# Sorting tokens by expert through DRAM in a four-stage transformer kernel

## The chip, the cores and the metric

The kernel runs on 1 core of one Trainium2 chip. The metric is the device time of one execution in microseconds (us), the median of several runs. The core has five engines with a queue of their own each: TensorE (PE in the rows; PEld is its weight load), VectorE (DVE), ScalarE (ACT), GpSimd (POOL) and SyncE (SP), which here only issues DMAs. A queue is worked off in order; engines wait for each other by semaphores.

## The reference

Input `x` is 64 sequences of 64 tokens of 128 numbers in float32, 4096 tokens in all, with a context of the same shape. Four residual sublayers follow each other, the last with the experts:

```python
x = x + tanh(g_xattn[0]) * L0_xattn(layernorm(x), ctx, ctx)        # 16 heads of 8, squared scores
x = x + tanh(g_ffn[0])   * L0_ffn(layernorm(x))                    # FP4-rounded gate/up/down, width 352
x = x + tanh(g_xattn[1]) * L1_xattn(layernorm(x), ctx, ctx, mask)  # one head, softmax
x = x + tanh(g_ffn[1])   * L1_ffn(layernorm(x))

def L1_ffn(src):
    x = ln(src + attention(src), ln1_g, ln1_b)       # 16 heads of 8, softmax
    gates = softmax(x @ gW + gb)                     # 8 experts
    w = the two largest gates of each token, 0 for the other six
    h = relu(einsum('nd,edf->enf', x, W1) + b1)      # 8 experts, 128 -> 256
    y = einsum('enf,efd->end', h, W2) + b2           # 256 -> 128
    return ln(x + einsum('ne,end->nd', w, y), ln2_g, ln2_b)
```

So only two of eight experts count for a token; which two depends on the data.

## The kernel before

**Groups and stages.** The 4096 tokens are worked in 8 groups of 512 (`N`), each four tiles (`T`) of 128 tokens. A group passes through stages whose names begin with a letter for their part: `a_` the first cross-attention, `f_` the FP4 feed-forward, `c_` the second cross-attention, `s_` the self-attention, the gate and the ranking, `e_` the experts and the output. Each engine has a function for each stage that it has a part in. The work of several groups is interleaved: a table `ORDER` at the end of the file lists, for each of the five queues, every stage with its group, as `e_hid.3:5` (piece 3 of group 5). This order is written out; nothing is decided at run time. Entries `w.N:0` of TensorE's list are fillers: N transposes of the identity into bank H, for no result (315 to 379 of them in the two kernels).

**Banks.** PSUM is cut into A2, A1 (parts a and f), B2, B1 (parts c and s), H and Y (the experts). `claim`, `filled` and `freed` turn a stage's place in TensorE's list into the semaphore value that a writer or a reader of its bank waits for.

**The norms.** Each of six norms per group takes four `bn_stats` on VectorE (`moments`), eleven small instructions on GpSimd (`factors`, one of them a power), and four activations on ScalarE (`normal`).

**The experts (dense).** `s_gate` computes gate logits, `s_rank` the softmax and for each token the rank of each expert, and `wgt`, the gate where the rank is 0 or 1 and 0 elsewhere. `s_gt` turns `wgt` for the product with the biases. Then each group goes through all 8 experts: `e_hid` k (16 of them) multiplies a half of an expert's first matrix, resident in `w1_s`, with all 512 tokens into H, and ScalarE takes it out with bias and relu into `hid`; `e_out` e makes 8 matmuls of 128 x 128 into Y, and VectorE adds them into `acc`, scaled by the token's weight for this expert:

```python
mm(H[:], w1_s[:, e, P * c:P * c + P], xmT[:, g % 2])                         # e_hid, 512 columns
mm(Y[:, P*t:P*t+P], hid[:, e % 2, c, P*t:P*t+P], w2_s[:, e, c, :], c == 0, c == FCH - 1)   # e_out
ve.scalar_tensor_tensor(out=acc[..t..], in0=Y[..t..], scalar=wgt[.., t, e:e+1], in1=acc[..t..], mult, add)
```

After the last expert follow the sixth norm (`e_n6`), a product on GpSimd (`e_z`), the sum with the residual (`e_fin`) and the store (`e_o`). A float32 matmul is two instructions in the profile, a transpose one. All matmuls go through one helper (L957), all plain ScalarE copies and activations through another (L468); so rows are told apart by their tiles. `pool` in the rows is the buffer that holds `hid` and `acc`.

Of the kernel before, what the change touches and what calls it, by code (L numbers as in the profile page):

```python
# [23 lines left out]
def flamingo_gated_stack(nc, x, ctx_in, mask, g_xattn, g_ffn,  # L24
# [6 lines left out]
    T = 4  # L31
# [15 lines left out]

    def tiles(ap):
        return ap.rearrange("b s d -> (b s) d").rearrange("(t p) d -> p t d", p=P)

    x_v, c_v, m_v, o_v = tiles(x), tiles(ctx_in), tiles(mask), tiles(out)

    ctx = ExitStack()
    with ctx:
# [15 lines left out]
        w1_s = sb("w1_s", [E, FCH * P])  # L70
# [37 lines left out]
        xax = sb("xax", [XB]); xsc = sb("xsc", [XB]); xrc = sb("xrc", [XB]); xqm = sb("xqm", [N])  # L108
# [3 lines left out]
        hqm = sb("hqm", [WID])  # L112
        th = sb("th", [2, I]); hh = sb("hh", [T, I])
        hqT = sb("hqT", [3, N])
# [5 lines left out]
        xs = sb("xs", [2, T, P])  # L120
        stats3 = sb("stats3", [T, 6]); hs3 = sb("hs3", [3, T]); rstd3 = sb("rstd3", [2, T])
        xn3 = sb("xn3", [T, P]); xT3 = sb("xT3", [N])
        q1T = sb("q1T", [N]); k1T = sb("k1T", [N]); v1s = sb("v1s", [T, P])
        keep = sb("keep", [T, S]); fill = sb("fill", [T, S])
# [6 lines left out]
        xT4 = sb("xT4", [N])  # L131
# [11 lines left out]
        xm = sb("xm", [T, P]); xmT = sb("xmT", [2, N]); wgt = sb("wgt", [2, T, E]); wT = sb("wT", [P])  # L143
        xb = sb("xb", [T, P])
        pool = sb("pool", [2 * FCH * N + 2 * N])
        hid = pool[:, 0:2 * FCH * N].rearrange("p (a c n) -> p a c n", a=2, c=FCH)
        acc = pool[:, 2 * FCH * N:2 * FCH * N + 2 * N].rearrange("p (a t d) -> p a t d", a=2, t=T)
# [34 lines left out]
        set1 = dict(A2=B2, A1=B1, qk=xmT[:].rearrange("p a (t d) -> p a t d", t=T), A0=P4, kT0=qT4, hT0=hT4,  # L182
# [7 lines left out]
        def bank_of(stage, g):  # L190
            b = BANK[stage]
            return {"A2": "B2", "A1": "B1"}[b] if stage[0] == "a" and g in OTHER else b

# [9 lines left out]
        setup = signal("setup"); p_b2 = signal("p_b2"); vset = signal("vset"); tanh = signal("tanh"); v_wq = signal("v_wq")  # L203
        x_wq = signal("x_wq"); x_qx = signal("x_qx"); x_qh = signal("x_qh")
        LOADS_W, LOADS_B, LOADS_O, LOADS_G, LOADS_F, LOADS_1, LOADS_E = 3, 3, 2, 2, 7, 18, 9
# [19 lines left out]
        v_out = signal("v_out")  # L225

# [14 lines left out]
        for stage, k, g in order("TensorE"):  # L241
            if stage in BANK and (stage, k) not in JOINED:
                bank_ = bank_of(stage, g)
# [4 lines left out]
        def claim(pe, stage, g, k=0):  # L248

            after(pe, free[bank_of(stage, g)], FREED[stage, k, g] - READERS.get(stage, 1))  # L250

        def filled(engine, stage, g, k=0):

            if g >= 0:
                engine.wait_ge(full[bank_of(stage, g)], FILLED[stage, k, g])

        def freed(engine, stage, g, k=0):

            if g >= 0:
                engine.wait_ge(free[bank_of(stage, g)], FREED[stage, k, g])  # L260
# [1240 lines left out]
```

## Time and profile before

| | |
|---|---|
| median of 3 runs | 723.52 us (722.88 to 726.53) |
| span of the profiled execution | 724.5 us (the page gives no other time for it) |
| TensorE busy | 673.4 us, 93% |
| VectorE busy | 516.0 us, 71% |
| ScalarE busy | 408.5 us, 56% |
| GpSimd busy | 265.6 us, 37% |
| DMA | 12.72 MB, mean 18 GB/s |

Busy times of different engines overlap. A row of the groups of instructions has: line, engine, operation, tile written <- tiles read, shape, count, then the busy time of the group and the mean duration of one, then the idle time of the engine ahead of it with what ended it. For TensorE the mean is longer than the step from one instruction to the next, since they are pipelined; the chain of waits shows the steps.

### The profile page before, as it was taken

Reading aid. Unit: us, or ns where it says so; the run is one execution under the profiler, and the core shown is the slowest. Engines: PE = TensorE matmul, PEld = TensorE weight load, DVE = VectorE, ACT = ScalarE, POOL = GpSimd, SP = SyncE. Lnnn points to the kernel's source line nnn. Section 1 sums busy time; section 2 is a strip of 40 time slices with the busy share of each in tenths; the row PEclk is TensorE's granted clock in tenths of the full one; section 3 lists DMA queues with packets and bytes.
Section 4 is the critical chain, followed back from the end, with each engine's and each line's share of the span. In section 5 each row is a group of like instructions: output and inputs, shape, how many; then the busy total and the mean of one; then the engine's idle time right before and its main releaser. Section 6 shows DMA issues by size and latency. Waiting matters only on the chain.

```text
span 724.5 us, 19854 instructions
## 1 busy us (share of the span) xinstructions
PE 673.4 (93%) x8416; PEld 496.8 (69%) x8416; DVE 516.0 (71%) x1085; ACT 408.5 (56%) x680; POOL 265.6 (37%) x624
## 2 busy tenths in 40 slices
PE   6898889998999999999999999999999999998983
PEld 6777676676677776777777777677676667566552
DVE  0928745997968787988897868878889765674432
ACT  2353665456755675758666765475747474644331
POOL 6023531085226335452455334352524125113202
PEclk8989999999999999999999999999999999999997
DMA  5510000100000010000000000000000000000000
GB/s 152 155 53 2 2 2 2 30 3 23 24 3 1 2 44 24 3 2 1 24 2 15 3 2 25 1 2 2 10 17 1 2 10 8 1 16 1 1 15 15
DMA packets 24023, 12.72 MB, mean 18 GB/s; under 512 B 6432, under 2 KB 23424, under 8 KB 23936
## 3 DMA queue, kind: packets, MB, share of 16 engines
q1 hardware_dynamic: 21888, 10.52, 5.3%
q8 instruction: 67, 1.10, 0.6%
q10 hardware_dynamic: 2048, 0.94, 0.5%
q14 instruction: 20, 0.16, 0.1%
HBM read 9.36 MB, written 2.10 MB: 16 GB/s over the span
## 4 chain that ended last, share of the span: by engine, by line
PE 78%; DVE 9%; ACT 6%; POOL 3%; issue 2%; DMA 1%; ACTq 1%; POOLq 0%; SPq 0%; DVEq 0%
PE B L957 18%; PE A L957 17%; PE Y L957 17%; PE H L957 15%; PE B L1214 4%; PE A L961 2%; PE B L961 2%; ACT pool L468 1%; ACT A L468 1%; PE A L1110 1%; POOL hs L366 1%; ACT xn L473 1%; DVE stats L680 1%; DVE hax L660 1%; DMA y<-in_L_xattn_Wq_w_dram 1%
## 5 line engine op out<-in xcount | busy, mean ns | idle before, releaser
L957 PE MATMUL H<-xmT,w_s 128*128 128x512 f32 x256 | 135.4, 611 | 6.4 <-ACT pool L468 6.4
L957 PEld LDWEIGHTS Y<-w_s,pool 128*128 128x128 f32 x1024 | 121.4, 192 | 20.2 <-issue 15.8
L468 ACT ACTIVATE pool<-H,b_s 128x512 f32<-128x512 f32 x128 | 87.7, 685 | 82.8 <-PE H L957 82.1
L957 PE MATMUL Y<-w_s,pool 128*128 128x128 f32 x1024 | 126.6, 277 | 2.5 <-ACT pool L468 1.6
L934 DVE SCALAR_TENSOR_TENSOR pool<-Y,wgt,pool 128x128 f32<-128x128 f32 x256 | 71.8, 343 | 46.8 <-PE Y L957 46.6
L356 POOL TENSOR_TENSOR hs<-stats 128x4 f32<-128x4 f32 x48 | 13.3, 278 | 237.1 <-DVE stats L680 236.9
L957 PEld LDWEIGHTS H<-xmT,w_s 128*128 128x128 f32 x256 | 40.0, 190 | 26.3 <-ACT pool L468 15.3
L875 DVE TENSOR_REDUCE mx<-B 128x16 f32<-128x1024 f32 x32 | 39.0, 1220 | 24.9 <-PE B L957 24.8
L966 PE MATMUL H<-ident 128*128 128x128 f32 x379 | 51.1, 286 | 1.7 <-POOL ident L341 1.7
L957 PE MATMUL B<-hT,qT 32*64 32x256 f32 (+1 forms) x640 | 47.6, 374 | 4.3 <-ACT P L468 1.0
L366 POOL TENSOR_TENSOR hs<-hs,mhalf 128x4 f32<-128x4 f32 x48 | 49.8, 1037 | 3.8
L966 PEld LDWEIGHTS H<-ident 128*128 128x128 f32 x379 | 45.4, 148 | 4.7 <-issue 2.6
L957 PE MATMUL A<-wguT,xTq 128*128 128x352 f32 x128 | 45.7, 481 | 2.0 <-DVE hh L783 1.8
L468 ACT ACTIVATE PT<-B 128x1024 f32<-128x1024 f32 x32 | 32.7, 1021 | 21.9 <-PE B L1214 21.8
L405 POOL TENSOR_TENSOR hh<-hh,hsc 128x1408 f32<-128x1408 f32 x6 | 15.5, 2589 | 77.1 <-DVE hh L673 77.1
L957 PE MATMUL A<-hT,kT 32*64 32x128 f32 x896 | 38.6, 283 | 4.5 <-ACT A L468 2.2
L468 ACT ACTIVATE P<-P 128x1024 f32<-128x1024 f32 x32 | 33.6, 1052 | 14.9 <-DVE P L877 14.9
L468 ACT ACTIVATE A<-A 128x1024 f32<-128x1024 f32 x28 | 28.6, 1021 | 20.9 <-PE A L957 20.9
L877 DVE TENSOR_TENSOR P<-B,mx 128x1024 f32<-128x1024 f32 x32 | 39.2, 1225 | 1.1
L957 PEld LDWEIGHTS A<-hT,kT 32*64 32x64 f32 x896 | 25.2, 132 | 19.4 <-PE A L957 6.8
L957 PEld LDWEIGHTS B<-hT,qT 32*64 32x64 f32 x640 | 17.2, 130 | 26.9 <-PE B L957 10.5
L882 DVE RECIPROCAL rc<-B 128x256 f32<-128x256 f32 x16 | 28.1, 1755 | 9.2 <-PE B L957 9.1
(232 smaller groups left out, 1371.0 us busy)
## 6 DMA issues: line engine op xcount, KB each, us to landing
xin<-in_x_dram SPq DMA_DIRECT2D x8, 256.0 KB, 3.6
out_dram<-xb SPq DMA_DIRECT2D x8, 256.0 KB, 2.3
cin<-in_ctx_dram SPq DMA_DIRECT2D x7, 256.0 KB, 3.0
w_s<-in_L_ffn_W_dram SPq DMA_DIRECT2D x1, 1024.0 KB
min_<-in_mask_BxSxS_ik_dram SPq DMA_DIRECT2D x8, 128.0 KB, 2.4
cin<-in_ctx_dram ACTq DMA_DIRECT2D x1, 256.0 KB, 4.3
hh<-in_L_ffn_w_down_dram ACTq DMA_DIRECT2D x1, 176.0 KB, 5.5
hh<-in_L_ffn_w_gate_dram ACTq DMA_DIRECT2D x2, 64.0 KB, 5.4
```

Source lines behind the costliest of these rows:

```text
L356: pl.tensor_tensor(w[:, 0], st[:, :, 1], st[:, :, 4], ALU.subtract)
L366: pl.tensor_tensor(w[:, 0], w[:, 0], mhalf[:], ALU.pow).then_inc(p_n[k], 1)
L405: pl.tensor_tensor(h, h, rep(hsc[:, 0:QB], 2, BLK), ALU.mult).then_inc(p_qh, 1)
L468: return act.activation(dst, source, f, **kw)
L875: ve.tensor_reduce(mx4[:, t % 2], by_s, AX.X, ALU.max).then_inc(v_mx, 1)
L877: ve.tensor_tensor(P4[:, t % 2].rearrange("p (h s) -> p h s", s=S), by_s, rep(mx4[:, t % 2], 2, S), ALU.subtract).then_inc(free["B2"], 1)
L882: ve.reciprocal(rc4[:], B1[:, N // 2:N]).then_inc(v_rc, 1)
L934: last = ve.scalar_tensor_tensor(out=acc[:, g % 2, t, :], in0=Y[:, P * t:P * t + P], scalar=wgt[:, g % 2, t, e:e + 1], in1=acc[:, g % 2, t ...
L957: return pe.matmul(o, l, r, start=start, stop=stop)
L961: last = pe.transpose(dst[:, P * t:P * t + P], source[:, t, :], ident[:])
L966: pe.transpose(H[:, 0:P], ident[:], ident[:])
L1214: last = pe.transpose(B2[:, P * pr:P * pr + P], P4[:, t % 2, a:a + P], ident[:])
```

## The change

The experts are computed only for the tokens that chose them. A group of 512 tokens makes 1024 token-expert pairs. They are sorted by expert into slots in DRAM, each expert's share beginning at a new tile of 128 slots; at most 15 tiles are needed, and always 15 are worked (`TILES`). `PARTS` says which groups are sorted together; here every group is by itself. Step by step:

- `i_cnt` (TensorE) counts, with products of 0/1 matrices, how many earlier tokens chose each expert; `s_rank` writes the 0/1 choices for it, and the two weights per token (`wk`).
- `i_pos` (VectorE, 17 small instructions) turns the counts into slot numbers `pos` and into the expert that owns each tile, `own`, and gathers its bias `b1t`.
- `i_sc` (GpSimd) writes each token's row of `xm` to its two slots: 8 indirect DMAs of 128 rows per group. `i_x` (SyncE) loads the sorted rows back, four tiles (a quad) at a time.
- `i_w` (SyncE) reads a tile's expert from `own` into a register and loads this expert's first matrix (128 KB) into one of 8 buffers (`w1t`); the resident `w1_s` is gone. The second matrices stay resident and are addressed by a register.
- `m_x` transposes a quad (TensorE, ScalarE), `m_h` makes the hidden layer, `m_y` the output; ScalarE copies it to SBUF and SyncE stores it to DRAM slots.
- `e_g` (GpSimd) gathers each token's two results: 8 indirect DMAs per group. `e_cmb` (VectorE) adds them, weighted, in place in `xm` (four buffers, `KEEP`). In the last group `m_` stages use two more banks in turn.
- To make room, several buffers are shared or single now: `xs`, `xT3` with `xT4`, `hqm` with `hqT`, `fill` with the mask, `xmT` with `xT0`. The residual of the output (`xs` plus a bias) goes out to DRAM (`r_st`) and comes back for `e_fin` (`r_ld`). Many stages get waits for the last reader of the buffer that they overwrite.
- The queues' orders are written anew. SyncE's list grows from 34 to 233 entries, GpSimd's from 104 to 165; TensorE's fillers go from 379 to 315.

The core of the diff:

```diff
+    TILES = [(2 * n * P + E * (P - 1)) // P for n in TG]
+    QUADS = [(n + 3) // 4 for n in TILES]
+    slots_x = [nc.dram_tensor("slots_x%d" % c, [TLM * P, D], F32) for c in range(2)]
+    slots_y = [nc.dram_tensor("slots_y%d" % c, [TILES[c] * P, D], F32) for c in range(CHUNKS)]
...
-        w1_s = sb("w1_s", [E, FCH * P])
+        w1t = sb("w1t", [NW, FCH * P])
...
+                def r_st(g, k):
+                    sp.wait_ge(p_xb, g + 1)
+                    sp.dma_start(r_v[:, g * T:g * T + T, :], xs[:]).then_inc(s_res, 16)
...
+                def i_w(c, j):
...
+                    e = sp.value_load(own[0:1, c % 2, j:j + 1], min_val=0, max_val=E - 1)
+                    sp.dma_start(w1t[:, n % NW, :], w1[bass.ds(e, 1)].rearrange("e d f -> d (e f)")).then_inc(ld_wt[n % NW], 16)
...
+                def i_x(c, q):
...
+                    sp.wait_ge(ld_sc[c], 32 * TG[c])
...
+                    sp.dma_start(xg[:, n % 2, 0:nt, :], slots_x[c % 2][4 * q * P:(4 * q + nt) * P, :].rearrange("(t p) d -> p t d", p=P))\
+                        .then_inc(ld_xg[n % 2], 16)
...
+                def m_y(c, q):
...
+                    sp.dma_start(slots_y[c][4 * q * P:(4 * q + nt) * P, :].rearrange("(t p) d -> p t d", p=P), yq[:, n % 2, 0:nt, :])\
+                        .then_inc(s_yq[n % 2], 16)
...
+                def i_sc(c, t):
...
+                    for k in range(2):
+                        pl.indirect_dma_start(out=slots_x[c % 2][:, :], out_offset=bass.IndirectOffsetOnAxis(ap=pos[:, c % 2, k, t:t + 1], axis=0),
+                                              in_=xm[:, g % KEEP, t % T, :], in_offset=None).then_inc(ld_sc[c], 16)
...
+                def e_g(g, t):
...
+                    for k in range(2):
+                        pl.indirect_dma_start(out=yg[:, k, t, :], out_offset=None, in_=slots_y[c][:, :],
+                                              in_offset=bass.IndirectOffsetOnAxis(ap=pos[:, c % 2, k, at_:at_ + 1], axis=0)).then_inc(ld_yg, 16)
...
-                def e_hid(g, k):
-                    e, c = divmod(k, FCH)
-                    filled(act, "e_hid", g, k)
-                    copy(hid[:, e % 2, c, :], H[:], ACT.Relu, bias=b1_s[:, e, c:c + 1]).then_inc(free["H"], 1)
+                def m_h(c, p):
...
+                    for j in range(2 * p, min(2 * p + 2, TILES[c])):
+                        for h in range(FCH):
+                            at_ = 2 * P * (j % 2) + P * h
+                            last = copy(hid[:, n % 2, j % 4, h, :], m_bank("m_h", c, p)[:, at_:at_ + P], ACT.Relu,
+                                        bias=b1t[:, c % 2, h, j:j + 1])
...
-                def e_out(g, e):
-                    filled(ve, "e_out", g, e)
+                def e_cmb(g, k):
...
+                    ve.wait_ge(ld_yg, 16 * 2 * T * (g + 1))
+                    for h in range(2):
+                        after(ve, v_cmb, 2 * g + h)
+                        for t in range(T):
+                            last = ve.scalar_tensor_tensor(out=xm[:, g % KEEP, t, :], in0=yg[:, h, t, :],
+                                                           scalar=wk[:, c % 2, h, first + t:first + t + 1],
+                                                           in1=xm[:, g % KEEP, t, :], op0=ALU.mult, op1=ALU.add)
...
+                def m_x(c, q):
+                    n = FIRST_Q[c] + q
+                    if q == 0:
+                        pe.wait_ge(v_i, INDEXED * c + INDEXED)
+                    for j in range(min(4, TILES[c] - 4 * q)):
+                        at_ = 4 * q + j
+                        owners[n % 2, j] = pe.value_load(own[0:1, c % 2, at_:at_ + 1], min_val=0, max_val=E - 1)
+                    pe.wait_ge(ld_xg[n % 2], 16 * (n // 2) + 16)
+                    claim(pe, "m_x", c, q)
...
+                            last = mm(m_bank("m_h", c, p)[:, at_:at_ + P], w1t[:, i % NW, P * h:P * h + P],
+                                      xgT[:, n % 2, P * (j % 4):P * (j % 4) + P])
...
+                            last = mm(m_bank("m_y", c, q)[:, P * j:P * j + P], hid[:, n % 2, j, h, :], w2_s[:, bass.ds(owners[n % 2, j], 1), h, :],
+                                      h == 0, h == FCH - 1)
...
+PARTS = ((0,), (1,), (2,), (3,), (4,), (5,), (6,), (7,))
```

The new TensorE queue ends, from the last attention output (`s_o4:7`) on: `m_x:6 e_bias:6 m_h:6 s_n5t:7 m_x.1:6 s_gate:7 m_h.1:6 m_y:6 m_x.2:6 i_cnt:7`, the rest of group 6's tiles with `s_gt:7` among them, then all tiles of group 7 and `e_bias:7`.

## Rows read from the trace of the kernel before

**Rows 1.** The page: span, busy time by engine.
```profile
span 724.5 us, 19854 instructions
...
PE 673.4 (93%) x8416; PEld 496.8 (69%) x8416; DVE 516.0 (71%) x1085; ACT 408.5 (56%) x680; POOL 265.6 (37%) x624
```

**Rows 2.** The page: chain that ended last, by engine and by line.
```profile
PE 78%; DVE 9%; ACT 6%; POOL 3%; issue 2%; DMA 1%; ACTq 1%; POOLq 0%; SPq 0%; DVEq 0%
PE B L957 18%; PE A L957 17%; PE Y L957 17%; PE H L957 15%; PE B L1214 4%; PE A L961 2%; PE B L961 2%; ACT pool L468 1%; ACT A L468 1%; PE A L1110 1%; POOL hs L366 1%; ACT xn L473 1%; DVE stats L680 1%; DVE hax L660 1%; DMA y<-in_L_xattn_Wq_w_dram 1%
```

**Rows 3.** Busy time by stretch: engines, granted TensorE clock, DMA share, GB/s.
```profile
0.00:20.00 20.00, 14.41 (x103) 13.07 (x104) 3.62 (x11) 4.16 (x9) 10.96 (x25) 0.83 0.57 147
...
60.00:100.00 40.00, 34.25 (x435) 27.21 (x434) 28.33 (x49) 23.62 (x41) 15.23 (x41) 0.96 0.01 1
...
300.00:400.00 100.00, 99.75 (x1281) 73.27 (x1281) 83.15 (x178) 66.85 (x119) 44.42 (x105) 1.00 0.03 8
...
680.00:724.00 44.00, 27.57 (x155) 18.60 (x154) 11.85 (x39) 12.00 (x21) 8.85 (x21) 0.92 0.04 12
```

**Rows 4.** Chain of waits in order of time: start, us, what; 640 to 725 us.
```profile
705.34 0.70 ACT pool L468
706.04 0.04 issue
...
707.21 1.78 PE Y L957 x16
708.99 0.88 PE H L957 x2
```

**Rows 5.** Groups of instructions on TensorE: hidden, output, fillers.
```profile
L957 PE MATMUL H<-xmT,w_s 128*128 128x512 f32 x256 | 135.4, 611 | 6.4 <-ACT pool L468 6.4
L957 PE MATMUL Y<-w_s,pool 128*128 128x128 f32 x1024 | 126.6, 277 | 2.5 <-ACT pool L468 1.6 <-DVE pool L934 0.9
L966 PE MATMUL H<-ident 128*128 128x128 f32 x379 | 51.1, 286 | 1.7 <-POOL ident L341 1.7
```

**Rows 6.** Groups on ScalarE and VectorE, shapes apart.
```profile
L468 ACT ACTIVATE pool<-H,b_s 128x512 f32<-128x512 f32 x128 | 87.7, 685 | 82.8 <-PE H L957 82.1
L473 ACT ACTIVATE xn<-xr,rstd 128x128 f32<-128x128 f32 x32 | 13.2, 484 | 12.1 <-POOL rstd L370 12.1
L468 ACT ACTIVATE xmT<-B 128x512 f32<-128x512 f32 x8 | 4.7, 593 | 4.1 <-PE B L961 4.1
L468 ACT ACTIVATE woT<-A 128x128 f32<-128x128 f32 x1 | 0.3, 259 | 0.0
L923 DVE SCALAR_TENSOR_TENSOR wgt<-rank,pe_ 128x32 f32<-128x32 f32 x8 | 1.5, 192 | 0.3
```

**Rows 7.** Group on VectorE: accumulation of an expert's output.
```profile
L934 DVE SCALAR_TENSOR_TENSOR pool<-Y,wgt,pool 128x128 f32<-128x128 f32 x256 | 71.8, 343 | 46.8 <-PE Y L957 46.6
```

**Rows 8.** Groups on GpSimd: the power in the norms, the longest instruction.
```profile
L366 POOL TENSOR_TENSOR hs<-hs,mhalf 128x4 f32<-128x4 f32 x48 | 49.8, 1037 | 3.8
L405 POOL TENSOR_TENSOR hh<-hh,hsc 128x1408 f32<-128x1408 f32 x6 | 15.5, 2589 | 77.1 <-DVE hh L673 77.1
```

**Rows 9.** DMA issues with landing; an issue's own time; a table load.
```profile
xin<-in_x_dram SPq DMA_DIRECT2D x8, 256.0 KB, 3.6
out_dram<-xb SPq DMA_DIRECT2D x8, 256.0 KB, 2.3
...
2.29 0.43 SPq L300 DMA_DIRECT2D y<-in_L_xattn_Wq_w_dram  x1
...
10.84 1.28 ACT L465 ACT_TABLE_LOAD   x1 [10.84 <-issue]
```

**Rows 10.** Timeline: last attention output, end of the ranking, last statistics.
```profile
660.40 1.06 PE L957 MATMUL B<-wdir,oT 128*128 128x128 f32 x8
...
677.33 0.19 DVE L923 SCALAR_TENSOR_TENSOR wgt<-rank,pe_ 128x32 f32<-128x32 f32 x1
...
713.88 0.87 DVE L680 BATCH_NORM_STATS2 stats<-pool 128x6 f32<-128x128 f32 x4
```

More of the change, by code:

```diff
@@ L46, in flamingo_gated_stack @@
     MAGIC = 1.5 * 2.0 ** 22
+    CHUNKS = len(PARTS)
+    PART = {g: c for c, part in enumerate(PARTS) for g in part}
+    TG = [T * len(part) for part in PARTS]
+    TILES = [(2 * n * P + E * (P - 1)) // P for n in TG]
+    QUADS = [(n + 3) // 4 for n in TILES]
+    FIRST = [sum(TILES[:c]) for c in range(CHUNKS)]
+    FIRST_Q = [sum(QUADS[:c]) for c in range(CHUNKS)]
+    TGM, TLM = max(TG), max(TILES)
+    LOADS_Z = 2 * ((TLM + 15) // 16)
+    KEEP = 4
+    NW = 8
     def tiles(ap):
@@ L510, in a_qt @@
                 def a_qt(g, k):
+                    if g == 0:
+                        act.wait_ge(vset, 3)
+                    filled(act, "a_s0", before(g), T - 1)
                     filled(act, "a_qt", g)
@@ L518, in a_av @@
                 def a_av(g, k):
+                    filled(act, "a_o0", before(g))
                     filled(act, "a_av", g)
@@ L582, in c_pt @@
                 def c_pt(g, k):
+                    filled(act, "c_av", g - 1)
+                    if g == 0:
+                        act.wait_ge(v_l2, norms(OTHER[0] + 1))
                     filled(act, "c_pt", g)
@@ L695, in a_k @@
                 def a_k(g, k):
+                    filled(ve, "a_kt", before(g))
+                    filled(ve, "a_qt", before(g))
                     filled(ve, "a_kv", g)
@@ L717, in a_q @@
                 def a_q(g, k):
+                    filled(ve, "a_kt", before(g))
+                    filled(ve, "a_qt", before(g))
                     filled(ve, "a_q", g)
@@ L824, in c_p @@
                 def c_p(g, k):
+                    filled(ve, "c_pt", g - 1)
                     ve.wait_ge(x_c, g + 1)
@@ L872, in s_s @@
                 def s_s(g, t):
+                    filled(ve, "s_t", *((g, t - 2) if t > 1 else (g - 1, t + 2)))
+                    if g == 0 and t == 0:
+                        filled(ve, "a_av", OTHER[0])
                     by_s = B2[:].rearrange("p (h s) -> p h s", s=S)
@@ L880, in s_o @@
                 def s_o(g, p):
+                    filled(ve, "s_o4", g - 1)
+                    if g == 0 and p == 0:
+                        filled(ve, "a_o0", OTHER[0])
                     filled(ve, "s_av", g, 2 * p)
@@ new lines, in i_cnt @@
+                def i_cnt(c, k):
+                    n = TG[c]
+                    skip = TGM - n
+                    pe.wait_ge(v_g, 16 * PARTS[c][-1] + 13)
+                    if c == 0:
+                        pe.wait_ge(p_ix, 7)
+                    claim(pe, "i_cnt", c)
+                    mm(Y[:, 0:n * E + E], before_m[:], flat(picked[:, skip:TGM + 1, :]), True, False)
+                    for t in range(n):
+                        last = mm(Y[:, (t + 1) * E:(n + 1) * E].rearrange("p (t e) -> p t e", e=E), ones_m[:],
+                                  rep(picked[:, skip + t, :], 1, n - t), False, t == n - 1)
+                    last.then_inc(full["Y"], 1)
@@ new lines, in m_y @@
+                def m_y(c, q):
+                    n = FIRST_Q[c] + q
+                    nt = min(4, TILES[c] - 4 * q)
+                    freed(pe, "m_h", c, (4 * q + nt - 1) // 2)
+                    claim(pe, "m_y", c, q)
+                    for j in range(nt):
+                        for h in range(FCH):
+                            last = mm(m_bank("m_y", c, q)[:, P * j:P * j + P], hid[:, n % 2, j, h, :], w2_s[:, bass.ds(owners[n % 2, j], 1), h, :],
+                                      h == 0, h == FCH - 1)
+                    last.then_inc(full[bank_of("m_y", c, q)], 1)
```

651 lines of the change are left out of this document (417 added, 234 removed).

## The prediction

> **What bounds the kernel now.** I read the page first. The span is 724.5 us, and the engines' busy times are 673.4 (TensorE), 516.0 (VectorE), 408.5 (ScalarE) and 265.6 (GpSimd) [rows 1]. The chain that ended last is 78% TensorE, and two banks of one helper line, Y and H, hold 17% and 15% of it [rows 2]: these are the expert matmuls. The stretches say when that holds. Between 300 and 400 us TensorE is busy 99.75 of 100 us and VectorE 83; from 60 to 100 us TensorE has only 34.25 of 40, and in the last 44 us 27.57 [rows 3]. So in the body what counts is TensorE work, and at the end a chain through all engines counts. The profile gives the span alone as its execution's time; the sum below is made against 724.5, which is 1.0 above the median of the runs (723.52).
>
> **What the experts cost.** For each group, every token goes through all 8 experts: 16 hidden matmuls of 512 columns and 64 output matmuls of 128 columns, each float32 matmul being two instructions. In the chain a hidden one (x2) takes 0.88 us and one expert's output (x16) 1.78 us, so one instruction of 128x128 by 128 columns takes 0.111 us at full clock [rows 4]. The chain's shares for Y and H on the helper line, 17.3% and 15.4%, are 237 us; less the bias products, 8 of the hidden shape at 0.87 = 7, the experts are 230 us. (The groups' own busy times, 126.6 and 135.4, include ends that lie under the next instruction [rows 5].)
>
> **After the change, per group.** 512 tokens x 2 choices in tiles that belong to one expert need at most 15 tiles, where the dense form has 32 tile-expert pairs. 15 tiles x (2 hidden + 2 output) x 2 instructions = 120, of the shape of the output matmuls: 13.3 us. 15 transposes at 0.13 (51.1 / 379 [rows 5]): 2.0. The count of positions, five small products, ten instructions at 0.1: 1.0. Together 16.3, for 8 groups 130. The queue has 315 fillers where there were 379, 64 x 0.135 = 8.6 less. Net TensorE: -230 + 130 - 8.6 = **-108.6 us**.
>
> **The other engines.** ScalarE loses 87.7 and gains, per group, 30 small activations at some 0.33 (between 0.259 and 0.484 [rows 6]), 4 copies in at 0.59 and 4 out at 0.59: 14.6 x 8 = 117, so 438 in all. VectorE loses 71.8 (256 accumulations at 0.28) and gains per group 8 accumulations at 0.28, five more small steps in the ranking and 17 in the placing at 0.19 [rows 6, 7], 6.4 in all: 516 - 72 + 51 = 495. Neither passes TensorE's 565, but in the 561 us up to the last attention output (below) VectorE now has about 480 to do, so an order of the queues that leaves gaps costs more than now. GpSimd gets 128 indirect DMAs (8 out, 8 back per group). The trace has none. Below stands a DMA issue on a hardware queue, 0.43 us [rows 9]; above, GpSimd's longest instruction, 2.59 [rows 8]. I take 1.04, the row of its slow small operation, since an indirect DMA is also work per partition in software: 128 x 1.04 = 133, GpSimd 399 in all, not the bound. But 8 of them in a row hold back what is queued behind them, above all the norms' factors, for which ScalarE and then TensorE wait; 8.3 us of such a hold costs nothing while another group's work lies in the queues, and that cover is thin at both ends.
>
> SyncE gets 120 expert loads of 128 KB, 32 tile loads, 32 tile stores, 16 transfers of the residual and 2 of zeros, about 202 issues x 0.43 = 87 us, and its queue waits in order. The bytes are 15.7 (weights) + 2 x 7.9 (tiles) + 8.4 (rows by index) + 4.2 (residual) + 2 (zeros) = 46 MB, 69 GB/s over 667 us; the first 20 us carry 147 GB/s [rows 3], so bandwidth is hidden. Single buffers in place of double ones (xs, xT3 with xT4, hqm with hqT, the mask with its fill) and the added waits for a reader cost nothing as long as the body is paced by TensorE; the residual must be stored before the next one is written, 1.3 + 2.3 us, under the fourth stage's attention.
>
> **Register loads.** Both TensorE and SyncE now read the tile's expert number into a register, 120 times each, and TensorE's queue waits behind each. The trace has no such load. Below stands the chain's gap of 0.04 us; above, the table load of ScalarE, 1.28, the only instruction here that fetches state; next below it a DMA issue at 0.43 [rows 4, 9]. I take 0.2, nearer to the issue, since four stand in a row and earlier matmuls still run: 24 us (bounds 5 and 154).
>
> The Trainium skill (DMA: Bandwidth & Descriptors, Latency and other measured facts) gives a load into registers a floor of about 600 ns, which unrolling by four amortizes. With 0.6 for each of 120 the estimate by that page is 72 us in place of 24, and the total 715; no row here shows it.
>
> **The end, step by step.** The last group's attention output leaves TensorE at 661.5 us, and 191 of the 230 us of expert work lie ahead of it (21 hidden and 11 output pieces, 39 us, behind). After: 661.5 - 191 + 6 groups x 16.3 + 1 - 8.6 = 561. From there to the end of the ranking the trace shows 661.5 to 677.5, 16.0 us [rows 10]. Then the count 1.1, nine placing steps 2.5, eight scatters 8.3, landing 2.3, the load of the tiles 3.6 [rows 9]: 34 us, of which TensorE fills only the 15.3 of group 6 and about 2 more. Then the experts of group 7, alone: TensorE 15.3, ScalarE 14.6, partly in turns, as the chain shows them now (0.70 of ScalarE between TensorE's pieces [rows 4]): 22. Then copy 0.6, store 2.3, eight gathers 8.3, landing 2.3, accumulations 2.2, and what follows now from the statistics at 713.9 to the end, 10.6 [rows 10]: 26.3. Sum: 561 + 34 + 22 + 26.3 = 643.3; with the register loads 667.3, against the runs' median **about 667**. So 57 us are gained, not 109: 27 are eaten by the way through DRAM at the end, 24 by the register loads.
>
> On landing, the Trainium skill (same page, Anatomy of one DMA) gives about 2.0 us plus the bytes at 436 GB/s, 2.2 for 64 KB as an estimate; the stores' 2.3 for 256 KB is near it, the loads' 3.6 above. That would leave the sum within 1 us.
>
> **The rivals.** (a) *The forecast*, 667, with its own range 635 to 700: chance 0.45. (b) *The register loads stall TensorE* at the price of the table load: 643 + 154 = 797. It decides from (723.5 - 643.3) / 120 = 0.67 us each; above that the kernel is slower. For it: a queue that waits for a fetch does nothing else. Against it: TensorE's own queue runs ahead by some instructions and the loads come before a wait anyway. Chance 0.13. (c) *GpSimd paces the body*: at 2.59 us per indirect DMA it has 265.6 + 332 = 597 us of work and the two ends grow by 16 x 1.55 = 25, so 692 at least; each group's six chains of factors (now 1.04 + eight small steps) queue behind 20 us blocks, and 8 x 4 us of that exposed gives 725. For it: GpSimd's waits are long today only because it is early. Chance 0.15. (d) *TensorE's work goes but the span doesn't follow*: VectorE at 495 us, more small dependent steps, a SyncE queue in order, single buffers. If the body packs like 60 to 100 us (0.86) and not like 300 to 400 (1.00), the 561 us become about 610, total 716; half of that, 690. Chance 0.17. (e) *Better than the sum*: loads at 0.04 and the early third, now 0.86 to 0.96 full, filled by the new order: 620 to 640. Chance 0.10. The granted clock is a part of all: it was 0.83 and 0.92 at the two ends, where TensorE was less busy [rows 3]; if the last 22 us of experts ran at 1.2 GHz, 15 us more.
>
> **Numbers.** Likeliest 667. Below 620 and above 728 I leave 0.04 and 0.15, so the range is 620 to 728. A change under 0.5% (3.6 us) can't be told from none here. Faster: all of (a) and (e), most of (d), half of (c), a little of (b): 0.77; same 0.04; slower 0.19.
>
> **What would show it.** TensorE busy near 565 us with 960 expert instructions at some 0.111 each; gaps of TensorE before the tile transposes in fours (register loads), 0.8 us if I am right, over 2.7 if (b); GpSimd's indirect DMAs at about 1 us each (over 2 if c), total near 400; a gap of TensorE of some 15 us ahead of the last group's experts and 26 us behind them; VectorE near 495. The prediction is wrong if TensorE's share of the chain falls under 60% in the body.

## The result and the profile after

The changed kernel takes **816.5 us** (median of four runs, 814.6 to 826.0); the kernel before, on the same chip, 725.0. The ratio is 1.128, 95% interval 1.122 to 1.135. The prediction was 667, range 620 to 728: the change makes the kernel 13% slower, not 8% faster, and the time lies outside the range.

The page of the changed kernel, to be read against [rows 1] and [rows 2]. In the slices, each digit is the busy share of 20.4 us in tenths, and for PEclk the granted clock:

```profile
span 816.4 us, 21791 instructions
...
PE 641.0 (79%) x8232; PEld 507.4 (62%) x8232; DVE 506.9 (62%) x1069; ACT 424.5 (52%) x856; POOL 413.1 (51%) x759
...
PE   3787988998988899989999889687876777666720
...
PEclk9979999999999999999679999979779899568775
...
PE 47%; DVE 18%; issue 11%; ACT 9%; POOL 8%; DMA 3%; SPq 1%; POOLq 0%; DVEq 0%; ACTq 0%
```

Three engines' busy times stand there nearly as priced: VectorE 507 (495), ScalarE 425 (438), GpSimd 413 (399). TensorE was to be busy near 565 us and is busy 641, 32 us less than before, at a mean granted clock of 0.891 instead of 0.983. The two products, 673.4 x 0.983 = 662 and 641.0 x 0.891 = 571, are a rough estimate of the work at full clock: some 91 us of it went (predicted 108.6). But TensorE's share of the chain fell from 78 to 47%, and "issue", time in which an engine waits for nothing that is shown, rose from 2 to 11%. The work went, and the span grew.

Where it grew is told by one marker, VectorE's reading of the last group's attention output. It came at 661.56 before. Here the marker stands at

```profile
709.38 0.69 DVE L1100 TENSOR_TENSOR y<-B,src 128x512 f32<-128x512 f32 x1 [2.26 <-PE B L1229]
```

**So the body, all that lies ahead of this marker, was to be 76 us shorter and is 48 us longer; the end, all behind it, grew from 63 to 107 us.** The stretches of the changed kernel (columns as in [rows 3]) show a TensorE that is never full and a clock that falls:

```profile
300.00:400.00 100.00, 89.38 (x1173) 70.79 (x1171) 75.64 (x152) 62.97 (x130) 49.59 (x77) 0.96 0.30 86
...
500.00:600.00 100.00, 80.53 (x820) 62.53 (x818) 59.18 (x126) 51.44 (x112) 54.67 (x78) 0.88 0.29 84
600.00:709.00 109.00, 78.50 (x1016) 64.72 (x1008) 53.56 (x135) 48.28 (x111) 50.09 (x86) 0.83 0.34 97
709.00:816.00 107.00, 51.01 (x299) 44.17 (x297) 25.73 (x81) 34.48 (x99) 43.97 (x72) 0.69 0.37 106
```

The costliest groups of the change (busy, mean ns of one, idle before and its releaser); the expert groups answer to [rows 5, 6], L1233 are the transposes of the tiles, L554 and L566 scatter and gather:

```profile
L566 POOL DMA_INDIRECT yg<-slots_y,pos x64 | 62.5, 977 | 42.9 <-issue 39.3
L1229 PE MATMUL H<-xgT,w1t 128*128 128x128 f32 x452 | 71.2, 305 | 14.6 <-ACT pool L597 9.0
L597 ACT ACTIVATE pool<-H,b1t 128x128 f32<-128x128 f32 x226 | 64.8, 370 | 33.8 <-PE H L1229 33.1
L554 POOL DMA_INDIRECT slots_x<-xm,pos x64 | 63.6, 994 | 35.4 <-issue 18.6
...
L1229 PE MATMUL Y<-w_s,pool 128*128 x452 | 66.6, 309 | 2.7 <-ACT pool L597 2.6
...
L1233 PE MATMUL H<-ident,xg 128*128 128x128 f32 x113 | 21.5, 318 | 48.1 <-issue 39.2
```

Ahead of these 113 transposes (the other seven of the 120 write bank A) TensorE is idle for 48.1 us in all, 39.2 of it "issue". That is where the four register loads of a quad stand. One such gap of 2.27 us in the timeline of TensorE:

```profile
449.07 0.63 PE L1229 MATMUL B<-PT,ones 128*32 128x64 f32 x32
451.97 0.30 PE L1233 MATMUL H<-ident,xg 128*128 128x128 f32 x1 [2.27 <-issue]
```

Four causes stood open. L: the register loads stall TensorE. C: the clock falls where TensorE waits, and that costs the time. H: a chain of waits that leads each group through all engines holds the body, whatever TensorE has to do. O: the changed order with its waits is slow in itself. G, a smaller one, is GpSimd's blocks of indirect DMAs.

### The profile page after: what moved, and what is told of

Same layout as the page of the kernel before. It is cut to its first block, busy times and chain, and to the rows that moved or that the text cites. A ratio compares the mean times of both kernels' runs of the same rounds, so it can differ in the third digit from the quotient of the medians.

```text
span 816.4 us, 21791 instructions
## 1 busy us (share of the span) xinstructions
PE 641.0 (79%) x8232; PEld 507.4 (62%) x8232; DVE 506.9 (62%) x1069; ACT 424.5 (52%) x856; POOL 413.1 (51%) x759
## 3 DMA queue, kind: packets, MB, share of 16 engines
q1 hardware_dynamic: 82192, 47.11, 20.4%
## 4 chain that ended last, share of the span: by engine, by line
PE 47%; DVE 18%; issue 11%; ACT 9%; POOL 8%; DMA 3%; SPq 1%; POOLq 0%; DVEq 0%; ACTq 0%
PE B L1229 13%; PE A L1229 12%; PE Y L1229 6%; PE H L1229 5%; ACT pool L597 3%; PE B L1486 3%; PE H L1233 2%; DVE mx L1081 2%; POOL hs L458 2%; DVE stats L870 2%; DVE P L1083 2%; ACT hT L614 1%; PE A L1233 1%; PE B L1233 1%; DVE rc L1091 1%
## 5 line engine op out<-in xcount | busy, mean ns | idle before, releaser
L566 POOL DMA_INDIRECT yg<-slots_y,pos x64 | 62.5, 977 | 42.9 <-issue 39.3
L1229 PE MATMUL H<-xgT,w1t 128*128 128x128 f32 x452 | 71.2, 305 | 14.6 <-ACT pool L597 9.0
L597 ACT ACTIVATE pool<-H,b1t 128x128 f32<-128x128 f32 x226 | 64.8, 370 | 33.8 <-PE H L1229 33.1
L554 POOL DMA_INDIRECT slots_x<-xm,pos x64 | 63.6, 994 | 35.4 <-issue 18.6
L1229 PEld LDWEIGHTS H<-xgT,w1t 128*128 128x128 f32 x452 | 62.7, 213 | 25.0 <-ACT pool L597 11.8
L1229 PE MATMUL Y<-w_s,pool 128*128 x452 | 66.6, 309 | 2.7 <-ACT pool L597 2.6
L1229 PEld LDWEIGHTS Y<-w_s,pool 128*128 128x128 f32 x452 | 63.6, 224 | 5.7 <-issue 5.1
L1233 PE MATMUL H<-ident,xg 128*128 128x128 f32 x113 | 21.5, 318 | 48.1 <-issue 39.2
L597 ACT ACTIVATE PT<-B 128x1024 f32<-128x1024 f32 x32 | 32.8, 1024 | 45.1 <-PE B L1486 44.7
L1229 PE MATMUL B<-hT,qT 32*64 32x256 f32 (+1 forms) x640 | 48.1, 378 | 7.7 <-ACT PT L597 2.8
L1233 PEld LDWEIGHTS H<-ident,xg 128*128 128x128 f32 x113 | 13.8, 159 | 55.6 <-issue 49.0
L1486 PE MATMUL B<-ident,P 128*128 128x128 f32 x256 | 36.9, 291 | 6.3 <-DVE P L1083 5.5
L597 ACT ACTIVATE A<-A 128x1024 f32<-128x1024 f32 x28 | 28.7, 1024 | 23.3 <-PE A L1229 23.1
L1205 DVE SCALAR_TENSOR_TENSOR xm<-yg,wk,xm 128x128 f32<-128x128 f32 x64 | 21.4, 396 | 30.7 <-DMA yg<-slots_y,pos 29.1
```

Source lines behind the costliest of these rows:

```text
L554: pl.indirect_dma_start(out=slots_x[c % 2][:, :], out_offset=bass.IndirectOffsetOnAxis(ap=pos[:, c % 2, k, t:t + 1], axis=0), in_=xm[:, g ...
L566: pl.indirect_dma_start(out=yg[:, k, t, :], out_offset=None, in_=slots_y[c][:, :], in_offset=bass.IndirectOffsetOnAxis(ap=pos[:, c % 2, k, ...
L597: return act.activation(dst, source, f, **kw)
L1205: last = ve.scalar_tensor_tensor(out=xm[:, g % KEEP, t, :], in0=yg[:, h, t, :], scalar=wk[:, c % 2, h, first + t:first + t + 1], in1=xm[:, ...
L1229: return pe.matmul(o, l, r, start=start, stop=stop)
L1233: last = pe.transpose(dst[:, P * t:P * t + P], source[:, t, :], ident[:])
```

## The experiments

All runs in one table. "Last output" is the marker above, in the profiled execution; the time is the median of the runs. So the two need not fit to the microsecond: the profiled execution of the changed kernel took 818.2 us, and e2's 783.7, e5's 682.9, e6's 696.3 and e13's 718.7, up to 5 us more than their medians. A kernel that lacks or changes part of the result is marked with a star, and its section says which part. The edits below are shown shortened.

| kernel | time | last output | from there to the end of the span |
|---|---|---|---|
| before | 725 | 662 | 63 |
| changed | 816.5 | 709 | 107 |
| e1 static experts in the output product * | 782.2 | 676 | 105 |
| e2 one load a quad, no checks | 778.4 | 679 | 103 |
| e11 one load a quad, with checks | 801.8 | 696 | 106 |
| e4 old order, no experts * | 697.0 | 658 | 38 |
| e5 the same, 4 fillers * | 679.5 | 643 | 38 |
| e6 the same, 12 fillers * | 692.5 | 656 | 39 |
| e9 as e5, no maxima * | 656.6 | 615 | 38 |
| e10 before, no maxima | 724.2 | 659 | 63 |
| e3 new order, no experts * | 723.5 | 678 | 46 |
| e13 the same, no placing * | 715.4 | 671 | 46 |
| e16 as e2, no maxima | 770.7 | 665 | 102 |
| e7 as e2, plain DMAs * | 768.1 | 671 | 95 |
| e8 as e2, no loads on SyncE * | 776.1 | 674 | 103 |
| e12 as e2, fillers at the end | 788.7 | 681 | 105 |
| e14, e15 as e2, light experts * | 781.6, 778.9 | 679, 677 | 101, 100 |
| e17 before, with 64 loads | 731.6 | 666 | 63 |
| e18 before, two banks at the end | 720.9 | 661 | 58 |

**e1: no register loads on TensorE.**

```
-  owners[n % 2, j] = pe.value_load(own[0:1, c % 2, at_:at_ + 1], min_val=0, max_val=E - 1)
+  owners[n % 2, j] = at_ % E          # and w2_s[:, owners[n % 2, j], h, :]
```

> Leaves out the 120 register loads on TensorE: the output product takes expert (tile number mod 8) instead of the tile's owner, so the output differs; everything else, the weight loads on SyncE and their register loads too, is as in the changed kernel. Theory L (the register loads stall TensorE, 49 us of waits ahead of the tiles' transposes, and the stalls let its clock fall): the waits ahead of the transposes fall under 15 us and the kernel takes 740 to 775 us. Rival O (the written order and the chain over SyncE, DRAM and GpSimd pace the kernel, TensorE would only wait elsewhere): 800 us or more, the idle time of TensorE stays above 150 us.

782.2 us, ratio to before 1.078 (1.077 to 1.080): 34 us shorter than the changed kernel, nearly all of it ahead of the last output (709 to 676). The tiles' transposes now wait 4.3 us in all, as L said, but the time lies between the two marks, above L's 775 and below O's 800: the loads are a part, not the cause. The products take another expert's second matrix, so the output differs.

**e2 and e11: one load instruction for four owners, without and with the checks of the bounds.** Both give the results of the changed kernel.

```
+  vals = nc.values_load_multi_w_load_instructions(own[0:1, c % 2, 4 * q:4 * q + nt], engines=[mybir.EngineType.PE],
+             min_val=0, max_val=E - 1, skip_runtime_bounds_check_because="...")[1]      (e11: without skip_...)
```

> The same results as the changed kernel: the four owners of a quad are loaded into TensorE's registers by one load instruction (32 loads in place of 120) and without the instructions that check their bounds (two for each owner). Theory L, if the cost sits in the loads and their checks: 49 us of waits fall to about 15 and the time comes to 770 to 790 us. Rival O: within 10 us of the changed kernel.

> The changed kernel with the four owners of a quad loaded by one load instruction (32 in place of 120), but with the two instructions for each owner that check its bounds left in. If the cost sits in the loads, it takes 778 to 785 us, as the run without the checks; if in the checks, 805 us or more.

778.4 and 801.8 us. From 120 loads to 32: 14.7 us, 0.17 for each load that went. Without the 240 checking instructions: another 23.4 us, 0.10 each. The 32 loads that stay in e2 cost nothing that shows: e1, with none, takes 782.2 us, no less than e2. The group of the tiles' transposes, e11 first, then e2:

```profile
L1233 PE MATMUL H<-ident,xg 128*128 128x128 f32 x113 | 21.7, 321 | 32.4 <-issue 24.7 <-DMA xg<-slots_x 4.8 <-ACT pool L597 2.7
```

```profile
L1233 PE MATMUL H<-ident,xg 128*128 128x128 f32 x113 | 19.6, 297 | 8.1 <-ACT pool L597 4.2 <-issue 2.6 <-DMA xg<-slots_x 0.9
```

The "issue" ahead of them goes 39.2, 24.7, 2.6. Loads and checks are 38 of the 91 us (34 by e1); e11 lay between its two marks, so neither loads nor checks alone are "the" cost. The other 53 us remain.

**e4 and e3: the body without experts, in the old and in the new order.** Taken out of the queues, in e4 the hidden and output products and the accumulations, in e3 scatter, gather, weight and tile transfers, the tile stages and the combining. Both lack the experts in their output.

```
- e_hid.*  e_out.*                             (e4, from before)
- m_x m_h m_y i_w i_x i_sc e_g e_cmb           (e3, from the changed kernel)
```

> The kernel before without its dense experts (no hidden products, no output products, no accumulates; the bias product stays), in the order of before. Its output lacks the experts. 665 us of TensorE's work at full clock less 230 is 435; with the idle time of start and end, 500 to 560 us. It is the measure for the body in the changed order: Theory O has it 40 us or more shorter than that one, theory L within 20.

> The changed kernel without its experts: no scatters, no weight loads, no tile transposes, no products, no gathers, no combining; routing, placing, the bias product and everything before them stay, in the changed order. Its output lacks the experts. TensorE's work left is about 450 us at full clock. Theory O (the order and the added waits are themselves slow): at least 40 us longer than the kernel before without its experts. Theory L: within 20 us of it, near 560 us.

697.0 us for e4 and 723.5 for e3, where 500 to 560 and about 560 were expected. e4 decides. **With no expert work at all, the body of before ends at 658 us instead of 662.** 230 us of TensorE's work go and 4 us come back; the whole is 28 us shorter, 25 of it at the end. TensorE is no longer full then, and its mean clock of 0.81 means that it had the lower of its two levels for 0.38 of the stretch (e4: its last output, then 220 to 640):

```profile
657.67 0.69 DVE L890 TENSOR_TENSOR y<-B,src 128x512 f32<-128x512 f32 x1 [2.24 <-PE B L957]
...
220.00:640.00 420.00, 317.01 (x4300) 220.61 (x4300) 284.20 (x516) 208.52 (x350) 166.53 (x392) 0.81 0.03 8
```

And e3's last output, at 678, is that of e2 and e1 (679, 676): leaving the experts out of the changed body gives nothing either. e3 takes 26.5 us more than e4, 20 of them ahead of the last output: between L's mark (within 20) and O's (40 or more). These 20 us don't build up evenly. Up to the output of the group before the last, e3 is 12 us behind e4 (603.6, 592.0); from there to the last output it loses 9 more. e2 against the kernel before shows the same: 7 us behind at that point (609.4, 602.7), 17 at the last output. In e3 too the clock is low, 0.78 from 220 to 640, and no run adds fillers to that body.

**e5 and e6: is it the clock?** Each hidden product of e4's kernel is replaced by 4 or 12 filler transposes.

```
- e_hid.0:0 ...
+ w.4:0 ...          (e6: w.12:0)
```

> The kernel before with each of its 128 hidden products replaced by four filler transposes of TensorE (512 of them, about 57 us at 0.11 us each), its output products and accumulates left out; its output lacks the experts. Without fillers this body took 697 us, its last attention output left at 658 and TensorE had a half clock for 161 us between 220 and 640. Theory C (the half clock makes the body slow where TensorE has too little to do): the clock comes back, the last attention output leaves before 625 and the kernel takes 640 to 670 us. Rival H (the body is held by the chain of products, reductions, exponentials and copies over the engines, whatever TensorE's load or clock): the last attention output stays at 650 to 662.

> As the run with four fillers, but twelve for each hidden product (1,536 fillers, about 170 us of TensorE, most of what the dense experts took): the clock should be full over the whole body. Theory C: TensorE's work is 435 + 170 = 605 us, so the last attention output leaves about 600 to 630 and the whole takes 650 to 680. Rival H: 650 to 662 for the last attention output, 690 to 700 for the whole, although the clock is full.

679.5 (its runs spread from 670 to 683, and the profiled one is the longest) and 692.5 us. With four the clock rises from 0.81 to 0.91 and the last output comes 15 us earlier; with twelve it is nearly full, 0.98, and the output is at 656 again (e5, then e6, the same stretch):

```profile
220.00:640.00 420.00, 342.70 (x4859) 252.35 (x4857) 290.87 (x521) 211.95 (x353) 169.50 (x394) 0.91 0.03 9
```

```profile
220.00:640.00 420.00, 387.68 (x5468) 316.87 (x5467) 287.13 (x523) 210.81 (x352) 167.84 (x395) 0.98 0.03 9
```

So the rise to 0.91 is worth 15 us or somewhat more in that body. e5's last output, 643, lies between the marks of C (before 625) and H (650 to 662); e6 is where H has it. Theory C falls as the main cause. What a full clock without fillers would give isn't shown, since the fillers take time of TensorE's queue themselves; e5's fastest run, 670.2 us at a mean clock of 0.933, suggests some microseconds more.

**e9 and e10: which chain?** The 32 reductions on VectorE that take the row maxima of the second attention are left out; zero is subtracted instead, which leaves the softmax the same up to rounding.

```
- ve.tensor_reduce(mx4[:, t % 2], by_s, AX.X, ALU.max).then_inc(v_mx, 1)
+ (mx4 set to 0 once)
```

> The old body with four fillers in place of each hidden product (680 us, last attention output at 643), without the 32 reductions of VectorE that take each row's maximum before the exponential of the second attention (1.22 us each, 39 us in all; zero is subtracted instead). It lacks the experts, as that run does. If the chain through VectorE sets the pace of the body (rival H), the last attention output leaves 20 to 39 us earlier, at 604 to 623; if something else paces it, under 8 us earlier.

> The kernel before, dense experts and all, without the same 32 maxima (zero is subtracted instead). Its TensorE is busy for 415 of the 420 us between 220 and 640. If TensorE is a second bound at the same place, the time hardly moves: 715 to 726. If TensorE's full row was only filled by what waited anyway, the time falls by 20 us or more, as in the body without experts.

656.6 us: 23 shorter than e5, last output 615 instead of 643. VectorE, busy only 69% of the body of e5 (290.87 of 420 us), stands in the chain that paces it. The same cut in the kernel before gives nothing (724.2, ratio 0.9988, 0.9973 to 1.0003), because there TensorE is full (e10, the same stretch):

```profile
220.00:640.00 420.00, 414.61 (x5191) 301.26 (x5192) 306.58 (x683) 264.94 (x444) 166.46 (x394) 1.00 0.03 9
```

**The body of before has two bounds at nearly the same place:** TensorE's work, and a chain of products, reductions, exponentials and copies that ends at 643 to 658 by itself. Take away either, the other stays. All these runs keep the written order of the attention and feed-forward stages, which was made with the experts in it; whether an order made for the body alone would end earlier wasn't tried.

**e16: the same cut in the sparse kernel** (e2's).

> The kernel of the run with one load a quad (778 us) without the 32 maxima of VectorE before the exponential of the second attention (39 us of VectorE, zero is subtracted instead). In the old body without experts this gave 23 us. If the changed kernel's body is held by the same chain: 15 to 30 us shorter. If it is held by TensorE, the loads or the queues of SyncE and GpSimd: under 8 us.

770.7 us. The last output comes 14 us earlier in the profiled executions (679, 665), but e2's was 5 us above its median; the medians differ by 7.7. That is half of the least that I expected of the chain, and just under the 8 us of its rival. So 39 us less of VectorE give the changed kernel a third of what they give e5's body: this chain is at most one part of what holds it, and the run doesn't say what the rest is.

**e13: the new body without the placing.** It lacks the experts, as e3.

```
- i_cnt (TensorE)   i_pos (VectorE, 17 instructions a group)
```

> The changed kernel's body without experts (723 us, last attention output at 678) also without the placing: the counting products on TensorE and the 16 VectorE instructions a group that turn counts into slots, owners and biases; it lacks the experts as that run does. VectorE is busy 35 us longer there than in the old order's body. If this bookkeeping on the queue of the chain makes the new body 20 us slower: last attention output at 660 to 668, the whole 10 us or more shorter. If the order and the added waits do: within 5 us of 723.

715.4 us, 8 shorter than e3, last output 671 instead of 678: between the two expectations. The runs of both spread (709 to 719, 718 to 726), so the size is rough. The placing, 33 us of VectorE, makes up about 7 of the 20 us; the other 13 are order, shared buffers and waits, which I didn't separate.

**e7 and e8: the queues of GpSimd and SyncE.**

```
- pl.indirect_dma_start(...)                   (e7)
+ pl.dma_start(slots_x[...fixed rows...], xm[:, g % KEEP, t % T, :])
- e = sp.value_load(own[...]); w1[bass.ds(e, 1)]   (e8)
+ w1[j % E]
```

> The kernel of the run with one load a quad (778 us), with each of the 128 indirect DMAs of GpSimd replaced by a plain DMA of the same tile to or from fixed slots, on the same queue; the rows go to other slots than the router says, so the output differs. Rival G (the blocks of eight indirect DMAs, 10 us of GpSimd each, hold the factors of the normalizations and the end): 20 us or more shorter. Theory L and rival O: within 10 us in the body; at the end the scatters and gathers of the last group give back at most 8 us.

> The kernel of the run with one load a quad (778 us), with the weight loads on SyncE issued for expert (tile number mod 8) without a register load: 120 register loads less on SyncE, the 120 weight DMAs stay; the products take another expert's first weights, so the output differs. If SyncE's queue, 1.1 us for each weight load, holds the rows of tokens and the results behind it: 15 us or more shorter, most of it after the last attention output. If not: within 5 us.

768.1 us (10 shorter than e2, half of the least that G asked for) and 776.1 (2 shorter, inside the spread). A plain DMA on GpSimd's queue takes 556 ns of it where the indirect one takes 977 to 994, 56 us less busy in all, and a fifth of that returns. In e7 other rows go through other slots, in e8 the products take another expert's weights.

**e12: the clock at the end.** 390 fillers in TensorE's order from the last cross attention on; results unchanged.

> The kernel of the run with one load a quad (778 us) with 390 filler transposes (43 us of TensorE at full clock) spread over TensorE's order from the last group's cross attention on, three before each attention or routing stage and six before each step of the experts, where TensorE waits and its clock was at half for 81 of the last 142 us. Theory C for the end (half clock doubles the products on the path): 10 to 20 us shorter. If the path is held by copies, transfers and the gathers: within 4 us, or longer by the fillers' own time.

788.7 us: 10 longer. The clock between 640 and 780 rose from 0.72 to 0.90 and the time too. That is the net of two things that this run can't part, what the clock gives back and what the fillers take (estimated at 43 us of TensorE's queue, 390 x 0.11). So C's 10 to 20 us didn't come; that the clock costs nothing at the end isn't shown. e2, then e12:

```profile
640.00:780.00 140.00, 78.57 (x711) 66.16 (x711) 46.74 (x136) 47.19 (x123) 61.51 (x97) 0.72 0.34 98
```

```profile
640.00:780.00 140.00, 95.92 (x1029) 84.43 (x1027) 49.77 (x136) 50.31 (x127) 61.62 (x97) 0.90 0.35 98
```

**e14 and e15: the experts of the last groups made light.** Of group 6, and then of 6 and 7, one hidden product in four, one output product in eight and one copy in four are left; the output of these groups is wrong.

> The kernel of the run with one load a quad (778 us) with the experts of group 6 cut to one product of eight on TensorE and one copy in four on ScalarE, all waits, transposes, loads, scatters and gathers kept; the output of that group is wrong. In its profile group 6's experts lie from 690 to 719 and group 7's transposes start at 719. If they alone hold group 7 back: 15 to 25 us shorter. If group 7's own routing and scatter (placing at 700, scatter 703 to 713, rows loaded about 717) end as late: within 5 us.

> As the run with group 6 cut, with group 7's experts cut in the same way. Group 7's experts took 28 us there (719 to 747), 16 of it products and 17 copies in turn. The cut one should leave about 10 us of transposes, weight and row loads and one copy a step: 15 to 18 us shorter than the run with group 6 alone; if the loads of weights or rows of SyncE set those 28 us, under 6 us shorter.

781.6 and 778.9 us: neither gets clearly shorter than e2's 778.4. Both lie at the mark that has something else hold the end (within 5, under 6). The chain of e15's kernel shows what stands there instead of the products (start, us, what):

```profile
715.14 3.30 DMA slots_y<-pool
718.43 8.40 issue
726.84 1.00 POOL yg L566
...
735.55 0.96 POOL yg L566
736.51 0.30 issue
736.82 2.49 DMA yg<-slots_y,pos
...
745.82 0.17 POOL rstd L462
745.99 0.31 issue
746.30 1.07 POOL yg L566
...
755.18 2.45 DMA yg<-slots_y,pos
```

The last results of group 6 are stored by SyncE only at 722.6, behind weight loads of group 7 and a residual load:

```profile
722.01 0.56 SPq L378 DMA_DIRECT2D xb<-res_d  x1
722.62 0.50 SPq L413 DMA_DIRECT2D slots_y<-pool  x1
```

Then GpSimd gathers group 6 (10 us), waits for the combining and computes group 6's factors, and only then gathers group 7, whose buffer yg is the same. From 726.8 to 757.6 that is 31 us that no faster expert shortens. With full experts, as in e2, the last product's copy ends at 747.5 and group 7's gathers start at 750.4; in e15, without most of the products, they start at 746.3. Two chains end side by side again.

**e17: the price of a load by itself**, in the kernel before, results the same.

```
+ owner = pe.value_load(own_all[0:1, e:e + 1], min_val=0, max_val=E - 1)   # ahead of each output product
- w2_s[:, e, c, :]
+ w2_s[:, bass.ds(owner, 1), c, :]
```

> The kernel before, with the expert of each of its 64 output products taken from a register: one load with two checks and an address of two steps ahead of each, on a TensorE that is busy 99% of the body. Same results. Theory L (a load with its checks is time of TensorE's queue, 0.3 us each by the 38 us of 120): 64 x 0.3 = 19, so 740 to 750 us. Rival: the queue runs ahead of the matmuls in flight and hides them: under 5 us more.

731.6 us, ratio 1.0077 (1.0053 to 1.0102): 5.5 us for 64 loads with their checks, 0.085 each, near the rival's mark and far from L's 19 us. In the waits of TensorE 3.0 us show:

```profile
PE Y L959 <- issue: 3.0, 10, 0.6
```

Singly between long rows of matmuls the same instructions cost a quarter of the 0.32 us that they cost in fours ahead of a transpose. That in the second case the matmuls in flight run out, and in the first not, fits both numbers; no run separates it from other reasons.

**e18: can the end be shortened?** The kernel before with the last group's hidden products in two banks in turn, results the same.

```
+ if stage == "e_hid" and g == GROUPS - 1 and k % 2:
+     return "A1"
```

> The kernel before, with the hidden products of the last group written in turn to two banks of PSUM (H and the one that the attentions no longer use) in place of one. Same results. In the chain of before, seven gaps of 0.78 us after the last attention output wait for the copy that frees the one bank: 7 x 0.78 = 5.5 us shorter, 717 to 721 us. If another chain of the last group (accumulates, norms) takes their place: within 2 us.

720.9 us, ratio 0.993 (0.991 to 0.995): 5.2 shorter, where 5.5 were summed. It beats both kernels.

## Why the prediction was wrong

**The step that failed is the 561:** "661.5 - 191 + 6 groups x 16.3 + 1 - 8.6". It turns TensorE's work into time in the body one for one. [Rows 3] gave the licence, 99.75 busy of 100; but a full row says only that TensorE is a bound, not that nothing else lies just behind. Measured without any expert, the last output comes at 658, four us earlier, where the same sum (661.5 - 191) gives 470. Of the 100 us that the sum took out of the body none came: with the cheap loads of e2 it ends at 679, with the changed kernel's at 709.

The rival for this, (d), "TensorE's work goes but the span doesn't follow", had the right mechanism with a chance of 0.17 and too small a price: I took its packing from another stretch, 0.86, and wrote 610. That doesn't come out of its own numbers: 561 / 0.86 is 652, and 758 in all, which is still 59 us short. Rows of busy time don't give 658 or 678; the chain has to be followed, one group through all engines, or measured without the work.

The terms one by one, against the forecast of 667, 149 us too low:
- **Body, without the loads' cost:** forecast 561, measured 679 (e2, in a profiled execution 5 us above its median): 118 of the 149. That is 17 us above before's own 662; between the two bodies without experts it is 20, of which e13 gives 7 to the placing. That single buffers and added waits "cost nothing as long as the body is paced by TensorE" failed by its own condition; order and waits hold about 13 us (e3 less e4 less placing).
- **Register loads:** forecast 24, measured 38 in the whole (changed less e2; 34 less e1), 0.32 each with their checks. 30 us of it lie in the body. Mechanism right, size 14 us too small. Rival (b)'s turning point, 0.67 each, was not reached. The Trainium skill (DMA: Bandwidth & Descriptors, Latency and other measured facts) says about 600 ns for a load and that four at once amortize it: as a price of each load this is nearly twice too high here. Its remedy, four at once, was worth 14.7 us in e11; the checks, which the page doesn't count, were the larger part.
- **GpSimd:** 1.04 for an indirect DMA, measured 0.98 and 0.99 plus 0.30 between two. Rival (c) asked for 2.59 each and isn't met; plain DMAs in their place give back 10 us (e7). The sum of the bytes, 46 MB, left out what the kernel moved before; the changed kernel's page has 57.8 MB at 71 GB/s. No run takes out the transfers alone, so what they cost isn't shown.
- **The end:** forecast 82 from the last output, measured 107 (103 in e2). The forecast's three pieces 34 + 22 + 26.3 came as 45 + 28 + 34. The first piece had 15.3 us of group 6's experts in it; in the trace they run until 752.6, and group 7's transposes start behind them, at 754.2. The forecast left out that one buffer yg and one GpSimd queue set the gathers in a row (e15), and that a store can wait behind loads on SyncE. Beginning at the last results' storing, the changed kernel's chain reads:

```profile
781.53 0.50 ACT pool L597
...
784.88 1.07 POOL yg L566
785.95 0.30 issue
...
793.75 2.45 DMA yg<-slots_y,pos
...
797.35 1.15 DVE xm L1205 x4
...
807.00 0.69 DVE xb L1217
```

- **The clock:** I named 15 us at the end for it, outside the sum. It did fall, to 0.69 over the end and 0.81 while group 7's experts ran (754 to 782); lifting it with fillers from 0.72 to 0.90 lengthened the kernel by 10 us (e12).
- **What was named as the sign of failure** was TensorE's share of the chain under 60% in the body. Added up from the chain between 220 and 640 us it is 48%, where the kernel before has 96%; over the whole span it is 47%.

Added up from before to after, in the profiled executions: body 17 (placing about 7, order and waits the rest) and 30 for the loads, end 44, together 92 with what is rounded off. **Open** stay which buffer or wait holds the 13 us of the new order, and why leaving out the maxima gives the sparse kernel a third of what it gives the body alone.

## What to carry to other kernels

An engine that is busy 99% of a stretch is a bound, but the gain of relieving it ends at the next one: before costing the change, run the kernel with that work left out altogether. Here such runs (697 of 725 us, 680 with a few fillers) say that, in this order of the stages, experts that cost nothing at all would have won 28 to 46 us. Load several values into registers with one instruction, away from the point where the queue runs dry, and leave out checks that the data's own clamp makes needless. At an end, look first at which buffer and which in-order queue set the last two groups one behind the other.

## What was not expected of the hardware

- The same register load with two checks cost 0.085 us of the span where it stood alone among matmuls (e17) and 0.32 in fours ahead of a transpose (changed less e2); each checking instruction weighed 0.10 (e11 less e2), more than half a load (0.17).
- A clock raised with fillers is no measure of time won: 0.81, 0.91 and 0.98 in the body (e4, e5, e6) gave last outputs at 658, 643 and 656, and 0.72 against 0.90 at the end (e2, e12) 778 and 789 us. The fillers' own time is in these numbers.
- GpSimd's queue is held 0.98 us by an indirect DMA of 64 KB (changed kernel) and 0.56 by a plain one (e7), with 0.30 us between two indirect ones.
